# Rotary rotations moved wholly to VectorE, softmax done in place, in a block of attention and experts

## The reference, cut to what matters

```python
h = x @ WA + bA
kv_lat, q_lat = jnp.split(h, 2, axis=-1)
kRt = _rope(h @ WB + bB, 0)            # one rotary key of 64 features, shared by all 16 heads
qRt = _rope(h @ WC + bC, 0)            # 1024 rotary query features = 16 heads x 64
q, k, v = q_lat @ WUQ, kv_lat @ WUK, kv_lat @ WUV      # per head, 128 wide
scores = (q . k + qRt . kRt) * dk ** (-0.5), causal
attn = jax.nn.softmax(scores, axis=-1)
out = (attn @ v) @ WZ + bZ
```

## Time and profile before

| what | value |
|---|---|
| median of 3 runs | 1962.95 us |
| the profiled execution | 1960.56 us |
| its span | 1958.6 us |
| PE busy | 1841.1 us (94%) |
| DVE busy | 946.0 us (48%) |
| POOL busy | 714.7 us (36%) |
| ACT busy | 627.6 us (32%) |
| mean granted clock of PE | 0.979 |

### The profile page before, as it was taken

How to read it: one execution, slowest core, us unless ns; L and a number is a source line. 1 busy time by engine, 2 the same in 40 slices (tenths; PEclk the granted TensorE clock), 3 DMA queues, 4 the chain that set the end, 5 groups by cost and what they waited for, 6 DMA issues and landing times. The chain is left out here.

```text
span 1958.6 us, 26874 instructions
## 1 busy us (share of the span) xinstructions
PE 1841.1 (94%) x9384; PEld 1429.4 (73%) x9384; DVE 946.0 (48%) x1589; ACT 627.6 (32%) x1088; POOL 714.7 (36%) x525
## 2 busy tenths in 40 slices
PE   6799999999999999999979997999999999999996
PEld 4577776767677676767757775888888888888885
DVE  4565656656665665666422476233334242423321
ACT  4333333333333332333222211333333333333331
POOL 1232222223221232323100004557566575757563
PEclk9999999999999999999979998999999999999998
DMA  7000101001010100101042212405212330422011
GB/s 254 22 1 17 48 5 59 0 27 37 16 48 5 59 0 16 48 6 58 12 112 87 86 65 93 144 0 150 75 32 63 109 85 0 113 101 43 0 21 22
DMA packets 69060, 104.88 MB, mean 54 GB/s; under 512 B 12320, under 2 KB 29472, under 8 KB 69024
## 3 DMA queue, kind: packets, MB, share of 16 engines
q1 hardware_dynamic: 49408, 77.70, 11.9%
q0 software_dynamic: 7200, 16.78, 4.8%
q10 hardware_dynamic: 12416, 9.92, 1.6%
HBM read 79.21 MB, written 25.17 MB: 53 GB/s over the span
## 5 line engine op out<-in xcount | busy, mean ns | idle before, releaser
L1847 DVE CAST hh<-hid 128x512 fp32r<-128x512 f32 x128 | 95.7, 748 | 438.7 <-ACT hid L1791 438.7
L1716 POOL TENSOR_TENSOR w1l<-w_raw,w1h 128x512 fp32r<-128x512 f32 x112 | 184.4, 1647 | 149.6 <-ACT w1h L1783 149.5
L431 POOL TENSOR_TENSOR prob<-prob,rinv 128x512 f32<-128x512 f32 x64 | 66.8, 1043 | 463.5 <-DVE rinv L692 463.5
L95 PE MATMUL bank_o<-Mh,mix_h 128*128 128x512 f32 x512 | 212.3, 415 | 2.3 <-DVE mix_l L663 1.4
L97 PE MATMUL bank_o<-Mh,mix_l 128*128 128x512 f32 x512 | 203.2, 397 | 0.0
L96 PE MATMUL bank_o<-Ml,mix_h 128*128 128x512 f32 x512 | 202.9, 396 | 0.0
L95 PE MATMUL e_h<-xh,w1h 128*128 (+1 forms) x512 | 200.9, 392 | 1.4 <-DVE xl L1858 1.4
L95 PE MATMUL e_y<-w2h,hh 128*128 128x512 f32 x512 | 200.6, 392 | 1.1 <-DVE hl L1849 0.7
L96 PE MATMUL e_h<-xl,w1h 128*128 (+1 forms) x512 | 200.2, 391 | 0.0
L97 PE MATMUL e_h<-xh,w1l 128*128 (+1 forms) x512 | 200.1, 391 | 0.0
L97 PE MATMUL e_y<-w2h,hl 128*128 128x512 f32 x512 | 199.4, 389 | 0.0
(11 more groups left out here) (279 smaller groups left out, 3554.5 us busy)
## 6 DMA issues: line engine op xcount, KB each, us to landing
w_raw<-in_W_dram SPq DMA_DIRECT2D x56, 512.0 KB, 4.2
stage<-in_x_dram SPq DMA_DIRECT2D x8, 1024.0 KB, 5.7
x_res<-in_x_dram SPq DMA_DIRECT2D x32, 256.0 KB, 2.6
out_dram<-x_res SPq DMA_DIRECT2D x32, 256.0 KB, 2.0
flat_dram<-flat_sb ACTq DMA_DIRECT2D x32, 256.0 KB, 2.0
rows<-out_dram SPq DMA_DIRECT2D x4, 1024.0 KB, 5.2
x_odd<-out_dram SPq DMA_DIRECT2D x4, 1024.0 KB, 5.4
stage<-in_W_dram SPq DMA_DIRECT2D x8, 512.0 KB, 5.3
```

What stands on the lines that cost most here:

```text
L95: nc.tensor.matmul(out, ah, bh, start=start and n == 0, stop=False)
L431: nc.gpsimd.tensor_tensor(prob[:, i % 2, :, :], prob[:, i % 2, :, :], rinv[:, :].unsqueeze(2).to_broadcast([P, HB, C]), ALU.mult).then_inc ...
L1716: nc.gpsimd.tensor_tensor(w1l[:, k, :, :], w1_at(pair, chunk), w1h[:, k, :, :].bitcast(F32), ALU.subtract).then_inc(S["w1_lo"], 1)
L1847: nc.vector.tensor_copy(hh[:, k, :], hid[:, k, :]).then_inc(S["h_hi"], 1)
```

## The change

All of a rotation's arithmetic goes to DVE. For the queries DVE does the cos multiply into `q_rope` directly behind the shuffle, then sin, then the addition; for the keys it does sin on `swapped`, cos in place on `raw`, and two additions that write `raw + swapped` into the two diagonal parts of `kblk`. The zeros of `kblk` are written once by a POOL memset in `absorb_weights`, and the keys' cos table loses its second half. ACT's eviction of query 0 now waits for the keys' additions, as these read raw; the other evictions wait for the shuffle and the cos multiply as before, which DVE now does. POOL's lists lose L416 and L424, so the gap between its other operations is gone. The tile `score` is gone: scores, maxima, subtraction and exp work in the step's half of `prob`, and L675's wait for the previous exp falls.

```diff
+            nc.gpsimd.memset(K["kblk"][:, :, :, :], 0.0)
...
-            def keys_cos(g):
-            def q_cos(g, u):
...
             def body(g, more):
                 gated(g, 2)
                 residual_bias(g, 0)
-                q_cos(g, 4)
-                q_cos(g, 5)
                 gated(g, 3)
                 residual_bias(g, 1)
-                q_cos(g, 6)
-                q_cos(g, 7)
                 residual_bias(g, 2)
                 gated(g, 4)
...
             def q_raw(g, u):
                 act.wait_ge(S["qr_mm"], g * NU + u + 1)
-                act.wait_ge(S["swap_ev"], g * NR + u + 1)
-                act.wait_ge(S["cos_ev"], g * NR + u + 1)
+                if u == 0:
+                    act.wait_ge(S["rope_done"], g * NR + 1)
+                else:
+                    act.wait_ge(S["swap_ev"], g * NR + u + 1)
+                    act.wait_ge(S["cos_ev"], g * NR + u + 1)
...
             def keys_rope(g):
                 r = g * NR
                 dve.wait_ge(S["lat_ev"], g * 2 + 2)
-                turn(r, K.parts["sink"])
+                swap_pairs(r)
+                dve.wait_ge(S["swap_ev"], r + 1)
+                by_table(swapped[:, :], swapped, K.parts["sink"]).then_inc(S["sin_ev"], 1)
+                by_table(raw[:, :], raw, K.parts["cosk"]).then_inc(S["cos_ev"], 1)
+                dve.wait_ge(S["sin_ev"], r + 1)
                 dve.wait_ge(S["cos_ev"], r + 1)
                 for h in range(2):
                     rows = slice(h * DR, (h + 1) * DR)
-                    last = nc.vector.tensor_tensor(kblk[rows, :, h, :], kblk[rows, :, h, :],
+                    last = nc.vector.tensor_tensor(kblk[rows, :, h, :], raw[rows, :].rearrange("p (b t) -> p b t", b=GB),
                                                    swapped[rows, :].rearrange("p (b t) -> p b t", b=GB), ALU.add)
                 last.then_inc(S["rope_done"], 1)
 
             def queries_rope(g, u):
                 r = g * NR + 1 + u
-                turn(r, K.parts["sinq"][:, u * C:(u + 1) * C])
+                q, table = q_rope[:, u % UB, :], slice(u * C, (u + 1) * C)
+                swap_pairs(r)
+                by_table(q, raw, K.parts["cosq"][:, table]).then_inc(S["cos_ev"], 1)
+                dve.wait_ge(S["swap_ev"], r + 1)
+                by_table(swapped[:, :], swapped, K.parts["sinq"][:, table]).then_inc(S["sin_ev"], 1)
                 dve.wait_ge(S["cos_ev"], r + 1)
-                nc.vector.tensor_tensor(q_rope[:, u % UB, :], q_rope[:, u % UB, :], swapped[:, :], ALU.add
-                                        ).then_inc(S["rope_done"], 1)
+                dve.wait_ge(S["sin_ev"], r + 1)
+                nc.vector.tensor_tensor(q, q, swapped[:, :], ALU.add).then_inc(S["rope_done"], 1)
...
-            def less_max(g, i, first=False):
+            def less_max(g, i):
                 n = g * STEPS + i + 1
+                row = prob[:, i % 2, :, :]
                 dve.wait_ge(S["s_mm"], n)
-                if not first:
-                    dve.wait_ge(S["exp_ev"], n - 1)
```

More of the change, by code:

```diff
@@ L56 @@
     "always": {"ident": P, "ones": P, "part": 1},
-    "attend": {"mask": C, "cosq": NU * C, "sinq": NU * C, "cosk": 2 * C, "sink": C},
+    "attend": {"mask": C, "cosq": NU * C, "sinq": NU * C, "cosk": C, "sink": C},
     "route": {"before": P, "iota": P, "adapter": 1, "tile": NT, "fold": NE, "trial": CANDS * TRIALS},
@@ L77, in const_columns @@
         "cosq": np.concatenate([c for c, _ in pairs], 1), "sinq": np.concatenate([s for _, s in pairs], 1),
-        "cosk": np.concatenate([cosk * (p[:, None] // DR == h) for h in range(2)], 1), "sink": sink,
+        "cosk": cosk, "sink": sink,
         "before": p[:, None] < p[None], "iota": np.broadcast_to(p[None], (P, P)), "adapter": p[:, None] // RANK,
@@ L344, in attention @@
         bias_sel = swapped[0:NSUB, :].rearrange("n (b d) -> n b d", b=GB)
-        score = sb("score", [P, HB, C])
         prob = sb("prob", [P, 2, HB, C])
@@ L438, in residual_bias @@
                                         ALU.add).then_inc(S["xres_biased"], 1)
[L440 to L443, removed]
             def first():
                 bias_rows(0)
-                project_front(0)
                 gated(0, 0)
@@ L468, in body @@
                 if more:
-                    project_front(g + 1)
                     gated(g + 1, 0)
@@ L515, in exps @@
                 act.wait_ge(S["sub_ev"], g * STEPS + i + 1)
-                nc.scalar.activation(prob[:, i % 2, :, :], score[:, :, :], ACT.Exp).then_inc(S["exp_ev"], 1)
+                nc.scalar.activation(prob[:, i % 2, :, :], prob[:, i % 2, :, :], ACT.Exp).then_inc(S["exp_ev"], 1)
             def prob_transposed(g, i):
@@ L627, in latent_lo, with by_table, swap_pairs @@
                                         ALU.subtract).then_inc(S["lat_lo"], 1)
-            def turn(r, sin):
+            def by_table(out, row, table):
+                return nc.vector.tensor_tensor(out.rearrange("p (b t) -> p b t", b=GB),
+                                               row[:, :].rearrange("p (b t) -> p b t", b=GB),
+                                               table.unsqueeze(1).to_broadcast([P, GB, C]), ALU.mult)
+            def swap_pairs(r):
                 dve.wait_ge(S["raw_ev"], r + 1)
@@ L635, in turn @@
                                          ).then_inc(S["swap_ev"], 1)
[L636 to L640, removed]
             def keys_rope(g):
@@ L668, in per_head @@
                 return row[:, :].unsqueeze(2).to_broadcast([P, HB, C])
-            def less_max(g, i, first=False):
+            def less_max(g, i):
                 n = g * STEPS + i + 1
+                row = prob[:, i % 2, :, :]
                 dve.wait_ge(S["s_mm"], n)
-                if not first:
-                    dve.wait_ge(S["exp_ev"], n - 1)
-                nc.vector.scalar_tensor_tensor(out=score[:, :, :],
-                                               in0=bank_s[i % 2][:, :].rearrange("p (h t) -> p h t", h=HB), scalar=SCALE,
-                                               in1=K.parts["mask"].unsqueeze(1).to_broadcast([P, HB, C]),
+                nc.vector.scalar_tensor_tensor(out=row, in0=bank_s[i % 2][:, :].rearrange("p (h t) -> p h t", h=HB),
+                                               scalar=SCALE, in1=K.parts["mask"].unsqueeze(1).to_broadcast([P, HB, C]),
                                                op0=ALU.mult, op1=ALU.add).then_inc(S["score_ev"], 1)
                 dve.wait_ge(S["score_ev"], n)
-                nc.vector.tensor_reduce(rmax[:, :], score[:, :, :], AX, ALU.max).then_inc(S["max_ev"], 1)
+                nc.vector.tensor_reduce(rmax[:, :], row, AX, ALU.max).then_inc(S["max_ev"], 1)
                 dve.wait_ge(S["max_ev"], n)
-                nc.vector.tensor_tensor(score[:, :, :], score[:, :, :], per_head(rmax),
-                                        ALU.subtract).then_inc(S["sub_ev"], 1)
+                nc.vector.tensor_tensor(row, row, per_head(rmax), ALU.subtract).then_inc(S["sub_ev"], 1)
             def softmax_sum(g, i, first=False):
@@ L718, in first @@
                     queries_rope(0, u)
-                less_max(0, 0, first=True)
+                less_max(0, 0)
                 softmax_sum(0, 0, first=True)
```

## The result

The changed kernel takes 2004.85 us, the median of 4 runs (2001.51 to 2005.15), against 1962.22 us for the kernel before in the same series: 42.6 us slower, a ratio of 1.022 (95% interval 1.0208 to 1.0232). The forecast was 1993 in a range of 1975 to 2006: right direction, 12 us short, and inside the range by 1 us. The profiled execution has a span of 2003.0 us, 44.4 above the one before.

A forecast was written before the change was run, and what follows sets the result against it. The bound was taken to be TensorE, 94% busy, waiting nearly only on the single raw tile's loop of evict, shuffle and cos, evict. 2.3 + 16.8 + 9.9 + 1.6 = 30.6 us gave 1993, range 1975 to 2006.

The forecast's parts named there:

- Front: At keys and queries 0 to 3, query 3's eviction comes 0.33 us later; over seven fronts 2.3 us.
- Middle: At queries 4 to 7, POOL holds up DVE and query 7's eviction comes 2.1 us later; over eight groups 16.8.
- rival A: In the middle, DVE's back-to-back cos and sin keep POOL out, only the last addition is held: 1981; chance 0.15.
- Rival B: In the middle, POOL's x_res additions don't hold DVE, leaving +0.1 there: not slower, 1966; chance 0.08.
- C: As Rival B, and the fronts' waits no longer cost clock (five falls, -8.3): faster, 1958; chance 0.05.
- Waits together: PE's added waits for the raw eviction: 2.3 us in the fronts and 16.8 in the middles, 19.1 forecast.
- The clock: PE's clock falls behind three in four middle waits, 1.65 us each (9.9), and once more in the fronts (1.6).
- rival D: In middles and fronts, new multiplies don't overlap (8 us), all middles and both clean fronts lose clock (+5): 2007; chance 0.12.
- the rule of the Trainium skill: Idle gaps between bursts return PE to its slow clock; by it all eight middles would pay, 13.2 us.
- Smaller ones: DVE busy about 30 us more in the changed profile; the softmax in place gains nothing.

The follow-up runs named there:

- keys-only kernel: The kernel before with only the keys rotated on DVE and the queries' cos still on POOL: 1956.6 us, ratio 0.9975 to the kernel before.
- two kernels without the additions in the way: The changed kernel with POOL's three x_res bias additions moved before step 3's prob multiply: 1984.82 us; with bias additions cut to 2 of 512 columns instead: 1968.32 us.
- filled waits: The changed kernel with 17 matmuls whose result nobody reads in PE's wait before the tenth key product: 1986.44 us, ratio 1.013 to the kernel before.

## Why the prediction was right, and where it was 12 us short

**Front: right.** +0.33 us was forecast for a steady front and +0.33 measured, with query 0's eviction at 3.63 behind the keys against the 3.65 worked out and a query period of 2.87. Over all eight fronts PE's waits rose by 3.8 us, forecast 2.3. The keys-only kernel shows that the front alone would have been better off without the queries' part.

**Middle: right.** +2.1 forecast, +2.17 measured in the third group, and 16.7 us more of PE's waits over the eight, forecast 16.8, through the chain that was named: cos, sin and the addition of query 5 at 1.01, 1.77 and 1.57 against 1.0, 1.6 and 1.7 forecast. The two kernels without the additions in the way (1984.8, 1968.3) rule out that the cost was DVE's length alone; the longer list without these hold-ups is worth about 7 us (ratio 1.0037). The prediction took the middle's wait as 1.94 us in all eight groups; the first had 1.69 and the eighth 0.36. Its sum came out because each grew by about as much (1.9 to 2.5 us).
So rival A (DVE's pair keeps POOL out) is wrong: sin, which had nothing left to wait for behind cos, took 1.77 us, POOL's addition having got in between. Rival B, and C that builds on it, fall with the same rows.

**Waits together: right.** PE's waits for the raw eviction rose from 42.5 to 63.0 us: 20.5, against 19.1 forecast.

**The clock: mis-sized.** The term was 9.9 + 1.6 = 11.5 us: three in four middles, 1.65 each, and one more fall in the fronts. Over stretches of 1 us from 60 us to the end of the attention, PE's busy time times what the clock lacked of full speed adds up to 9.9 us in the kernel before and 34.9 in the changed one: 25.0 us. With the waits that makes 45.5, and the span grew by 44.4. The share of middles was 8 of 8, and the price of a fall wasn't always that of one. The prediction took a fall that comes within the wait to be cheaper. Three came so, in the first, second and fifth group (from 605.0 to 605.7 PE did nothing, its wait ended at 605.72, and the clock was 0.75 on average), and they were the dear ones: the clock stayed low for about 7 us, and they cost 2.4, 3.1 and 3.2 us, the other five 1.7 each. All eight middles together are 17.3 us. The other 7.7 us are falls in the fronts: nine from 60 us on outside the middles where there had been six. All seven later fronts have one where five had, and two are long (3.1 us each, in the fourth and seventh group).
The trace had these prices only for waits up to 2.2 us. The prediction let the clock cost 0 to 14.8 us; it cost 25.0. With its own upper ends, 2.3 + 8 x 2.6 + 14.8, it would have reached 2001 us. That the result lies inside the range is luck: the upper end had been set just below rival D's time. Rival D had the falls right, all middles and both clean fronts, and came within 2 us of the time, but 8 us of it were for what didn't happen: the new multiplies do overlap (sin starts at 356.94, before cos's end at 357.01), and the long falls were not in it.
On the rule of the Trainium skill (TensorE: Matmul & The Clock Gate, "HAM oscillation"), by which every middle would pay: this trace agrees, with a fall behind the seven waits of about 4 us and also behind the eighth group's 2.25.

**Smaller ones.** DVE's busy time rose by 12 us, not 30. By groups of instructions it is 24: the cos multiplies bring 51.6, the sin multiplies lose 18.2 and the keys' additions 8.0, as less of their time is hold-up, and the rest 1.3. The other 12 us are overlap, which the page counts once: each query's cos starts about 0.1 us before the shuffle's end, and its sin about as much before the end of cos. Softmax in place at nothing: right.

## What to carry to other kernels

A unit of work moved onto the engine with the shorter list can be a loss where a buffer ties it into a loop of three engines: write out the loop (evict, read, read, evict) and count the period before and after. With a second buffer, and the x_res addition put before query 6, the same move went from +42 us to between -13 and -16. The two edits were not tried apart for the kernel with every cos on POOL, nor the x_res addition alone with one tile. And a wait of a few us on TensorE can cost twice, once as a wait and once as slow matmuls behind it: here 20.5 us of waits brought 25.0 us of low clock. When one wait is taken away, look in the same engine's list for what is ordered behind it, since that is the next one.

## What the runs showed of the hardware that was not expected

A low clock doesn't end with the first busy us behind a wait: after the 4 us waits it was over within 4 us in some groups and took about 7 in others, with the same instructions (363 to 367 against 605 to 613). The three middles and two fronts in which it took 7 were those in which the clock had fallen before PE's wait ended. Behind the filled waits it stayed at 1.00.

The length of the last wait doesn't settle whether the clock falls: waits of 1.91 to 1.95 us in the middle went without a fall six times of six in the kernel before, and with one five times of six in the keys-only kernel. Which of them pays is not explained by these runs.

DVE and POOL let each other in after single instructions, also between two DVE instructions with nothing left to wait for. An operation of DVE with two inputs in SBUF that starts while one of POOL's runs ends 0.54 to 0.56 us behind it (all 66 of the 128x512 ones in the attention of the kernel before), whatever its own start. Where DVE's had started first it took its 0.69 us (40 query additions), and POOL's behind it was the longer one: at 298.29 DVE's addition took 0.69, and POOL's multiply from 298.57 took 1.56 us, where 1.29 is its shortest. DVE's additions to x_res, which read one input from PSUM, took 0.64 to 0.69 us beside POOL's operations too.
